# Attention row maxima turned by TensorE in f32 inside a product with V, and split from PSUM

## The chip, the cores and the metric

The kernel runs on one core of a Trainium2 chip. The metric is the device time of one execution in microseconds (us). TensorE (PE) multiplies matrices; VectorE (DVE), ScalarE (ACT) and GpSimd (POOL) compute; SyncE (SP) issues DMAs. Each engine runs its own list of instructions in order, and semaphores tie the lists together.

## The reference

```python
xn = _layernorm(x, axis=-1)                       # x: 8 x 512 x 512, f32
q, k, v = (proj(Wq), proj(Wk), proj(Wv))          # 16 heads of 32
q, k = _apply_rope(q, k)
scores = jnp.einsum('bhqd,bhkd->bhqk', q, k) / sqrt(32)
scores = jnp.where(causal, scores, finfo.min)
attn = jax.nn.softmax(scores, axis=-1)
out = jnp.einsum('bhqk,bhkd->bhqd', attn, v) ... @ Wo.T
# experts: top 2 of 8 by xn @ gate_w.T, softmax of the two as weights
y = sum over the two of (xn @ expert_w[e].T + expert_b[e]) * weight
return x + out + y
```

## The kernel before, in words

The attention is cut into 32 steps: one for each of 8 batches and 4 groups of 4 heads (`N = 32`). Step `n` on PE holds pieces of several steps' work, in an order written by hand in `step(n)`:

- `scores(n + 1, k)`, k = 0 to 10 (L959, L961): scores of the next step, queries on partitions, in two PSUM banks by turns. Their only use is the largest score of each row. `largest_score(n + 1, k)` on DVE (L1463) reduces each bank to columns of `top`, 128 partitions by 16 values (4 heads, 4 blocks of queries). Unit `k` waits until the maximum of unit `k - 2` is taken.
- `shifted_scores(n, k)`, k = 0 to 10 (L977): scores of this step the other way round, keys on partitions, with two more rows in the operands which subtract the row maximum. ACT takes the exponential of each (`exps`, L756) into `pT`. PE's unit waits for the exponential two units back.
- `times_v(n, j)` (L990, L993): exponentials by V, and by ones for the sums. It waits for `masked`: POOL zeroes the diagonal blocks (L590) when the exponentials of block j are there. `times_v(n, 0)` and `(n, 1)` are in step n, `(n, 2)` and `(n, 3)` in step n + 1.
- projections: Q and K of step n + 3 (L1027), V (L1036), the output projection (L1051). DVE rotates Q and K out of PSUM (L1447, L1448), POOL finishes them (L581, L582), ACT and POOL split them in two f16 halves (L741, L586), SP stores them and loads them back stacked.

The row maxima reach the two extra rows of Q in this way. After unit 10, `split_c` on DVE scales `top` by 2^-14 in f32 (L1471), again into f16 as the high half (L1472), and writes the difference as the low half (L1473): `c_hl`, 128 by 32 in f16. `turn_c` on PE (L966) turns it to 32 by 128 in PSUM; it stands behind `shifted_scores(n, 7)` and the last 6 passes of `project_v`. `copy_c` on ACT (L763), behind the eighth exponential, copies it to `c_turn`, 32 by 128. `move_c` on SP stores `c_turn` to memory (L411) and loads it as the two rows (L413). SP's later transfers of the step queue up behind `move_c`: K stored and stacked, and, at the head of the next step, in some steps the load of another batch of x.

Before step 0 the same is done once by a prologue with its own order. On DVE there: the last maxima, `split_c(0)`, `rotate(1, 2)`, `stats_of(1)` (layer norm of batch 1), `scale_of`, `rstd_of(1)`. On ACT there: `high_qk(1, 2)`, `copy_c(0)`, `take_v(1)`, `std_of(1)`, and `scale_x_for_pe(1)`, which waits for `rstd_of(1)`; then V tiles 2 and 3 are copied, for which PE's first `shifted_scores` waits.

Some steps carry more. In steps 2, 3, 5, 6, 8, 9 (`TURN_AT`) DVE turns four blocks of x (L1409), two of them among the last maxima. In steps 1, 2, 3, 5, 6, 8, 9, 10, 11 a weight matrix is split: `high_w` on ACT (L732) ahead of the eighth exponential and `low_w` on DVE (L1326). At step 11 (`CHOOSE`) DVE picks the experts (`choose(1)`, L1345 to L1354), and PE's `ranks` (L901) at the end of that step waits for it. Between steps 15 and 16 PE does the experts (L942). In steps 16 to 30 DVE adds experts' results to two output tiles a step (`add_experts`, L1507, L1508).

## Time and profile before

| | us |
|---|---|
| median of 3 runs | 1005.34 (1003.37, 1005.34, 1011.82) |
| the profiled execution's own time | 1008.12 |
| its span, first to last instruction | 1006.3 |
| PE busy | 932.0 |
| DVE busy | 743.2 |
| POOL busy | 565.7 |
| ACT busy | 435.2 |
| experts' stage on PE, about | 457 to 667 |

The granted TensorE clock was 0.982 of full on average. In the chain of work that ended last PE has 67%, DVE 12%, DMA 7%, POOL 6%. A step of the last stage, counted from the first `shifted_scores` of one step to that of the next, takes 21.05 us (841.14 to 862.19). Times in the rows are counted from the span's start; the duration of a row is from the first instruction's start to the last one's end, and PE's instructions overlap, so that the time a piece of PE's work takes is better read from start to start.

### The profile page before, as it was taken

How to read it: one execution, taken by the hardware profiler on the slowest of the kernel's cores; microseconds unless marked ns; L12 is line 12 of the kernel's file. 1: busy time of each engine (PE TensorE's matmuls, PEld its weight loads, DVE VectorE, ACT ScalarE, POOL GpSimd, SP SyncE). 2: the span in 40 equal slices, each digit the busy share in tenths (PEclk: the TensorE clock that was granted, in tenths of full speed). 3: DMA queues.
4: the chain of work that ended last, by engine and by line, in shares of the span. 5: the costliest groups of instructions: out<-in, count | busy, mean ns of one | idle time of the engine just before them, and what ended most of it. 6: DMA issues, size and time to landing. Idle time of an engine off the chain costs nothing.

```text
span 1006.3 us, 18752 instructions
## 1 busy us (share of the span) xinstructions
PE 932.0 (93%) x6589; PEld 447.7 (44%) x6589; DVE 743.2 (74%) x1322; ACT 435.2 (43%) x711; POOL 565.7 (56%) x557
## 2 busy tenths in 40 slices
PE   2899989989999978988999999989999999999887
PEld 1344434434444433444555555544444444444333
DVE  7888988888889899543444444477878888788865
ACT  5367866666765432331211211214433444334442
POOL 1545675664676548572333333237887788777651
PEclk9999999999999999998999999999999999999999
DMA  6366588788785352385555555554555554455431
GB/s 238 106 220 223 146 278 311 204 300 292 206 291 209 117 210 85 134 309 177 179 168 176 179 170 174 168 214 142 184 159 176 191 191 148 148 181 179 157 107 54
DMA packets 107964, 188.63 MB, mean 187 GB/s; under 512 B 11873, under 2 KB 65249, under 8 KB 102625
## 3 DMA queue, kind: packets, MB, share of 16 engines
q1 hardware_dynamic: 97072, 152.03, 44.5%
q0 software_dynamic: 10800, 35.40, 12.3%
q8 instruction: 56, 0.92, 0.4%
q14 instruction: 36, 0.29, 0.1%
HBM read 117.13 MB, written 70.25 MB: 186 GB/s over the span
## 4 chain that ended last, share of the span: by engine, by line
PE 67%; DVE 12%; DMA 7%; POOL 6%; ACT 4%; issue 3%; SPq 1%; another core or an unknown queue 0%; DVEq 0%; ACTq 0%; POOLq 0%
PE psum L942 18%; PE psum L1027 11%; PE psum L1036 6%; PE psum L1051 6%; PE psum L990 6%; PE psum L977 5%; PE psum L959 5%; PE psum L993 5%; DMA x_in<-x 3%; PE psum L919 3%; DVE top L1463 3%; PE psum L961 2%; POOL gT L571 1%; DMA c_rows<-c_turn 1%; POOL y_in L616 1%
## 5 line engine op out<-in xcount | busy, mean ns | idle before, releaser
L756 ACT ACTIVATE pT<-psum,factors 128x512 f32<-128x512 f32 (+1 forms) x352 | 219.6, 640 | 267.6 <-PE psum L977 239.3
L1463 DVE TENSOR_REDUCE top<-psum 128x1 f32<-128x384 f32 (+3 forms) x352 | 210.7, 635 | 24.1 <-PE psum L961 23.1
L1027 PE MATMUL psum<-xT,w_att 128*128 128x512 f16 x768 | 199.0, 385 | 6.9 <-DVE xT L1414 4.8
L942 PE MATMUL psum<-w_exp,x_gT 128*128 x852 | 197.4, 382 | 0.8 <-DVE x_gT L1419 0.6
L959 PE MATMUL psum<-k_stack,q_stack 96*128 96x384 f16 (+3 forms) x512 | 129.1, 305 | 22.2 <-DVE top L1463 21.4
L606 POOL DMA_INDIRECT x_g<-xn_rows,tok_of x71 | 67.3, 948 | 143.8 <-PE psum L919 136.4
L977 PE MATMUL psum<-q_stack,k_stack 98*128 98x256 f16 (+3 forms) x512 | 129.5, 306 | 6.3 <-ACT pT L756 5.0
L1419 DVE TENSOR_TENSOR x_gT<-psum,x_gT 128x512 f16<-128x512 f32 x71 | 49.0, 692 | 106.9 <-ACT x_gT L780 94.4
L942 PEld LDWEIGHTS psum<-w_exp,x_gT 128*128 128x128 f16 x852 | 83.9, 98 | 87.4 <-issue 3.9
L780 ACT ACTIVATE x_gT<-psum 128x512 f16<-128x512 f32 x71 | 42.3, 597 | 173.2 <-PE psum L919 173.1
L590 POOL TENSOR_SCALAR_AFFINE_SELECT pT<-pT 128x512 f32<-128x512 f32 x128 | 99.3, 785 | 18.7 <-ACT pT L756 18.7
L1027 PEld LDWEIGHTS psum<-xT,w_att 128*128 128x128 f16 x768 | 70.8, 99 | 75.2 <-issue 6.9
L990 PE MATMUL psum<-pT,v_sb 128*32 128x512 f32 (+1 forms) x992 | 93.3, 448 | 7.6 <-POOL pT L590 7.2
L596 POOL TENSOR_TENSOR o_hl<-o_sb,o_hl 128x512 f16<-128x512 f32 x31 | 36.5, 1176 | 112.0 <-ACT o_hl L770 112.0
L1051 PE MATMUL psum<-w_att,o_hl 128*128 128x512 f16 x384 | 98.1, 380 | 1.3 <-DVE o_hl L1500 1.3
L1036 PE MATMUL psum<-w_att,xT 128*128 128x512 f16 x384 | 98.6, 382 | 0.0
L993 PE MATMUL psum<-pT,ones 128*32 128x512 f32 (+1 forms) x992 | 90.4, 436 | 0.0
L961 PE MATMUL psum<-causal,ident 128*128 128x128 bf16 (+2 forms) x352 | 87.0, 247 | 0.0
L959 PEld LDWEIGHTS psum<-k_stack,q_stack 96*128 96x128 f16 x512 | 46.7, 98 | 78.2 <-DVE top L1463 40.3
L977 PEld LDWEIGHTS psum<-q_stack,k_stack 98*128 98x128 f16 x512 | 44.5, 98 | 80.4 <-issue 33.1
L616 POOL DMA_INDIRECT y_in<-y_rows,idx_y x64 | 66.0, 1032 | 19.7 <-issue 11.6
L1433 DVE SCALAR_TENSOR_TENSOR y_sb<-psum,down,bias_all 128x512 f32<-128x512 f32 x71 | 53.3, 751 | 17.7 <-issue 15.8
(172 smaller groups left out, 1283.9 us busy)
## 6 DMA issues: line engine op xcount, KB each, us to landing
y_rows<-y_sb SPq DMA_DIRECT2D x71, 256.0 KB
w_in<-w_all SPq DMA_DIRECT2D x12, 1024.0 KB, 9.6
q_stack<-qk_rows SPq DMA_DIRECT2D x96, 128.0 KB
k_stack<-qk_rows SPq DMA_DIRECT2D x96, 128.0 KB
x_in<-x SPq DMA_DIRECT2D x8, 1024.0 KB, 13.5
qk_rows<-q_hl SPq DMA_DIRECT2D x32, 256.0 KB, 2.2
qk_rows<-k_hl SPq DMA_DIRECT2D x32, 256.0 KB
xn_rows<-x_in SPq DMA_DIRECT2D x8, 1024.0 KB, 4.7
```

Of the source, the lines that this page charges most:

```text
L590: pool.affine_select(out=p_diagonal(j), in_=p_diagonal(j), compare_op=ALU.is_ge, fill=0.0, base=0, pattern=[[0, HG], [1, P]], channel_mult ...
L756: act.activation(p_of(j, h, heads), banks[BANK_T + (NT_ * n + k) % 2][:, 0:W], ACT.Exp, scale=factors[:, 0:1]).then_inc(exp_done, 1)
L942: now = pe.matmul(banks[s % 4], x_gT[s % 4][:, xp * C + c, :], w_exp[:, bass.ds(e, 1), wp, c, :].rearrange("p e d -> p (e d)"), start=n == ...
L959: pe.matmul(bank[:, h * W:(h + 1) * W], q_stack[u][0:ROW_C, h0 + h, i * P:(i + 1) * P], k_stack[u][0:ROW_C, h0 + h, 0:W], start=h == 0, st ...
L961: pe.matmul(bank[:, 0:heads * W].rearrange("p (h t) -> p h t", h=heads)[:, :, W - P:W], ident16[:], causal[:, 0:heads, :], start=False, st ...
L977: now = pe.matmul(bank[:, h * W:(h + 1) * W], k_stack[u][0:ROW_C + 2, h0 + h, j * P:(j + 1) * P], q_stack[u][0:ROW_C + 2, h0 + h, j * P:S] ...
L990: pe.matmul(banks[BANK_O][h * HD:(h + 1) * HD, j * P:S], v_sb[b % 2][:, j, g * P + h * HD:g * P + (h + 1) * HD], p_of(j, h, 1), start=j == ...
L993: now = pe.matmul(banks[BANK_DEN][h * HD:(h + 1) * HD, j * P:S], ones32[:], p_of(j, h, 1), start=j == 0, stop=j == J - 1)
L1027: now = pe.matmul(bank, w_att[:, what, wp, c, g * P:(g + 1) * P], xT[b % 2][:, xp * C + c, :], start=at_pass == 0, stop=at_pass == 3 * C - 1)
L1036: now = pe.matmul(banks[bank], xT[b % 2][:, xp * C + c, j * P:(j + 1) * P], w_att[:, 2, wp, c, :], start=at_pass == 0, stop=at_pass == 3 * ...
L1051: now = pe.matmul(banks[bank], o_hl[b % 2][:, c, xp, j * P:(j + 1) * P], w_att[:, 3, wp, c, :], start=at_pass == 0, stop=at_pass == 3 * C - 1)
L1463: return dve.tensor_reduce(out=top[:, h:h + heads, i], in_=banks[BANK_S + k % 2][:, 0:heads * W].rearrange("p (h t) -> p h t", h=heads), a ...
```

## The change

The split on DVE in front of the turn goes, with its three tiles `c_scale`, `c_f`, `c_hl`. PE turns `top` itself in f32 (16 by 128), inside `times_v(n, 0)`, behind the 4 products with V and ahead of the 4 with ones. ACT, now ahead of the eighth exponential, writes the high half from PSUM with the scale; DVE writes the low half from PSUM. `c_turn` becomes 16 by 2 by 128. DVE's `low_c` stands behind a block turn, a `low_w` or one tile of `add_experts` in the steps which have one, and directly behind the last maximum in the others.

```diff
-    c_turn = at("c_turn", [2 * HG * J, P], F16)
+    c_turn = at("c_turn", [HG * J, 2, P], F16)
...
             def move_c(m):
-                sp.wait_ge(c_copied, m + 1)
-                sp.dma_start(c_rows[m].rearrange("f (r t) -> (f r) t", t=P), c_turn[:]).then_inc(c_stored, 16)
+                sp.wait_ge(c_lo, m + 1)
+                sp.dma_start(c_rows[m].rearrange("f (r t) -> r f t", t=P), c_turn[:]).then_inc(c_stored, 16)
...
-            def copy_c(m):
+            def high_c(m):
                 act.wait_ge(c_turned, m + 1)
                 if m:
                     act.wait_ge(c_stored, 16 * m)
-                act.activation(c_turn[:], half(BANK_S + 1)[0:2 * HG * J, 0:P], ACT.Copy).then_inc(c_copied, 1)
+                act.activation(c_turn[:, 0, :], banks[BANK_S + 1][0:HG * J, 0:P], ACT.Copy, scale=2.0 ** -LOG_C).then_inc(c_hi, 1)
...
+                if n + 1 < N:
+                    high_c(n + 1)
                 exps(n, 7)
-                if n + 1 < N:
-                    copy_c(n + 1)
...
             def turn_c(m):
-                pe.wait_ge(c_made, m + 1)
-                pe.transpose(half(BANK_S + 1)[0:2 * HG * J, 0:P], c_hl[:].rearrange("p f r -> p (f r)"), ident16[:]).then_inc(c_turned, 1)
+                pe.wait_ge(max_done, NS * (m + 1))
+                pe.transpose(banks[BANK_S + 1][0:HG * J, 0:P], top[:].rearrange("p h i -> p (h i)"), ident32[:]).then_inc(c_turned, 1)
...
+                if j == 0 and n + 1 < N:
+                    turn_c(n + 1)
                 for h in range(HG):
                     now = pe.matmul(banks[BANK_DEN][h * HD:(h + 1) * HD, j * P:S], ones32[:], p_of(j, h, 1),
...
-                if nxt:
-                    turn_c(n + 1)
                 shifted_scores(n, 8)
...
-            def split_c(m):
-                dve.wait_ge(max_done, NS * (m + 1))
-                if m:
-                    dve.wait_ge(c_turned, m)
-                tops = top[:].rearrange("p h i -> p (h i)")
-                dve.tensor_tensor(c_f[:], tops, c_scale[:], ALU.mult)
-                own.link(dve.tensor_tensor(c_hl[:, 0, :], tops, c_scale[:], ALU.mult))
-                dve.tensor_tensor(c_hl[:, 1, :], c_f[:], c_hl[:, 0, :], ALU.subtract).then_inc(c_made, 1)
+            def low_c(m):
+                dve.wait_ge(c_hi, m + 1)
+                dve.scalar_tensor_tensor(c_turn[:, 1, :], banks[BANK_S + 1][0:HG * J, 0:P], 2.0 ** -LOG_C, c_turn[:, 0, :],
+                                         ALU.mult, ALU.subtract).then_inc(c_lo, 1)
...
                     largest_score(n + 1, 10)
-                    split_c(n + 1)
                 if n in TURN_AT:
                     turn_blk(TURN_AT[n], 2)
+                elif n - 1 in JOB_AT:
+                    low_w(JOB_AT[n - 1])
+                for w in late_tiles(n)[:1]:
+                    add_experts(w)
+                if nxt:
+                    low_c(n + 1)
+                if n in TURN_AT:
                     turn_blk(TURN_AT[n], 3)
                 if n == CHOOSE:
                     choose(1)
-                if n - 1 in JOB_AT:
+                if n in TURN_AT and n - 1 in JOB_AT:
                     low_w(JOB_AT[n - 1])
...
-            split_c(0)
             rotate(1, 2)
+            low_c(0)
             stats_of(1)
```

On DVE in the prologue, before the first step, the order was this (each name is the tile written, then what it is read from; `stats` is `stats_of(1)`):

```order
L1463 TENSOR_REDUCE top<-psum 128x1 x7
L1471 TENSOR_TENSOR c_f<-top,c_scale 128x16
L1472 TENSOR_TENSOR c_hl<-top,c_scale 128x16
L1473 TENSOR_TENSOR c_hl<-c_f,c_hl 128x16
L1447 STREAM_SHUFFLE turned_k<-psum 128x512
L1448 TENSOR_TENSOR plain_k<-psum,trig_sb 128x512
L1286 BN_STATS stats<-x_in_143 128x6 x4
```

and is now this (the file's lines are 3 to 7 fewer for the same code):

```order
L1460 TENSOR_REDUCE top<-psum 128x1 x7
L1444 STREAM_SHUFFLE turned_k<-psum 128x512
L1445 TENSOR_TENSOR plain_k<-psum,trig_sb 128x512
L1465 SCALAR_TENSOR_TENSOR c_turn<-psum,c_turn 16x128
L1283 BN_STATS stats<-x_in_139 128x6 x4
```

The write of the low half, which waits for ACT, stands in front of the statistics of batch 1; the three instructions of the split waited for DVE alone.

On PE around `times_v(n, 0)` the order was:

```order
L1036 MATMUL psum<-w_att,xT_136 128x512 x3
L990 MATMUL psum<-pT,v_sb_103 32x512 x4
L993 MATMUL psum<-pT,ones_54 32x512 x4
L977 MATMUL psum<-q_stack_97,k_stack_100 128x384
L1036 MATMUL psum<-w_att,xT_136 128x512 x6
L966 MATMUL psum<-ident_49,c_hl 32x128
L977 MATMUL psum<-q_stack_97,k_stack_100 128x256 x4
```

and is now:

```order
L1035 MATMUL psum<-w_att,xT_133 128x512 x3
L987 MATMUL psum<-pT,v_sb_100 32x512 x4
L963 MATMUL psum<-ident_50,top 16x128
L992 MATMUL psum<-pT,ones_54 32x512 x4
L974 MATMUL psum<-q_stack_94,k_stack_97 128x384
L1035 MATMUL psum<-w_att,xT_133 128x512 x6
L974 MATMUL psum<-q_stack_94,k_stack_97 128x256 x4
```

The turn is now ahead of the products with ones, one `shifted_scores` and six passes of `project_v`.

On DVE at the end of step 11 (`best` to `gap` is `choose(1)`, `w_hl` is `low_w`) the order was:

```order
L1463 TENSOR_REDUCE top<-psum 128x1 x2
L1471 TENSOR_TENSOR c_f<-top,c_scale 128x16
L1472 TENSOR_TENSOR c_hl<-top,c_scale 128x16
L1473 TENSOR_TENSOR c_hl<-c_f,c_hl 128x16
L1345 TENSOR_REDUCE best<-rest 128x32
...
L1353 TENSOR_TENSOR chosen<-one_hot_152,one_hot_153 128x256
L1354 TENSOR_TENSOR gap<-best 128x32
L1326 SCALAR_TENSOR_TENSOR w_hl<-w_in_140,up,w_hl 128x2048
```

and is now:

```order
L1460 TENSOR_REDUCE top<-psum 128x1 x2
L1323 SCALAR_TENSOR_TENSOR w_hl<-w_in_137,up,w_hl 128x2048
L1465 SCALAR_TENSOR_TENSOR c_turn<-psum,c_turn 16x128
L1342 TENSOR_REDUCE best<-rest 128x32
...
L1350 TENSOR_TENSOR chosen<-one_hot_149,one_hot_150 128x256
L1351 TENSOR_TENSOR gap<-best 128x32
```

The choice of experts stands behind the low half of a weight matrix and of the maxima, and no longer ahead of it.

## Rows read from the trace of the kernel before

**Rows 1.** A stretch: its us; busy PE, PEld, DVE, ACT, POOL (instructions); PE clock; DMA.

```profile
693.00:925.00 232.00, 232.00 (x1732) 106.98 (x1728) 193.33 (x320) 98.72 (x176) 184.77 (x187) 1.00 0.55 172
```

**Rows 2.** Waits, whole run: us in total, times, longest.

```profile
PE psum L959 <- DVE top L1463: 21.4, 15, 3.1
```

**Rows 3.** Timeline of PE in step 24: start us, us, instruction.

```profile
849.65 1.06 PE L990 MATMUL psum<-pT,v_sb 128*32 128x512 f32 x8
850.53 1.04 PE L993 MATMUL psum<-pT,ones 128*32 128x512 f32 x8
851.51 0.34 PE L977 MATMUL psum<-q_stack,k_stack 98*128 98x384 f16 x1
851.68 1.46 PE L1036 MATMUL psum<-w_att,xT 128*128 128x512 f16 x6
853.07 0.23 PE L966 MATMUL psum<-ident,c_hl 128*32 128x128 f16 x1
853.23 0.39 PE L977 MATMUL psum<-q_stack,k_stack 98*128 98x256 f16 x2
```

**Rows 4.** Timeline of PE around an f32 turn ahead of 32-wide products.

```profile
246.95 0.27 PE L896 MATMUL psum<-ident,amax 128*128 128x128 f32 x1
247.15 0.64 PE L990 MATMUL psum<-pT,v_sb 128*32 128x256 f32 x8
```

**Rows 5.** Groups by line and shape: count, busy us, mean ns, idle before.

```profile
L1473 DVE TENSOR_TENSOR c_hl<-c_f,c_hl 128x16 f16<-128x16 f32 x32 | 33.6, 1051 | 1.1
...
L1471 DVE TENSOR_TENSOR c_f<-top,c_scale 128x16 f32<-128x16 f32 x32 | 13.2, 412 | 1.1
...
L1472 DVE TENSOR_TENSOR c_hl<-top,c_scale 128x16 f16<-128x16 f32 x32 | 5.2, 163 | 0.0
```

**Rows 6.** Timeline of the prologue: DVE, ACT, PE; idle time and its releaser in brackets.

```profile
53.94 2.46 DVE L1286 BATCH_NORM_STATS2 stats<-x_in 128x6 f32<-128x512 f32 x4
...
57.28 0.25 ACT L763 ACTIVATE c_turn<-psum 32x128 f16<-32x128 f16 x1
...
59.45 2.92 ACT L698 ACTIVATE x_p<-x_in,shift,rstd 128x512 f32<-128x512 f32 x4 [1.14 <-DVE shift L1302]
...
63.40 0.39 PE L977 MATMUL psum<-q_stack,k_stack 98*128 98x512 f16 x1 [1.08 <-ACT v_sb L748]
```

**Rows 7.** Timeline of step 11: ACT's high half of a weight, DVE's choice, PE's ranks.

```profile
326.59 2.00 ACT L732 ACTIVATE w_hl<-w_in,up 128x2048 f16<-128x2048 f32 x1
...
328.23 0.41 DVE L1345 TENSOR_REDUCE best<-rest 128x32 f32<-128x256 f32 x1
...
331.62 0.43 DVE L1353 TENSOR_TENSOR chosen<-one_hot,one_hot 128x256 f16<-128x256 f32 x1
...
334.53 0.95 PE L901 MATMUL psum<-chosen,ones 128*128 128x8 f16 x32
```

**Rows 8.** Timeline of step 5: PE's product with ones, DVE, POOL.

```profile
187.32 1.04 PE L993 MATMUL psum<-pT,ones 128*32 128x512 f32 x8
...
187.42 0.65 DVE L1463 TENSOR_REDUCE top<-psum 128x1 f32<-128x512 f32 x1
...
191.00 2.30 DVE L1326 SCALAR_TENSOR_TENSOR w_hl<-w_in,up,w_hl 128x2048 f16<-128x2048 f32 x1
...
192.09 2.23 POOL L586 TENSOR_TENSOR k_hl<-plain_k,k_hl 128x512 f16<-128x512 f32 x1 [1.68 <-ACT k_hl L741]
```

**Rows 9.** The chain that ended last, pieces in order: start us, us, what.

```profile
144.11 4.34 DMA c_rows<-c_turn
...
154.78 15.12 DMA x_in<-x
```

**Rows 10.** Timeline of step 24: DVE, POOL, and PE's second product with V.

```profile
848.80 1.28 DVE L1463 TENSOR_REDUCE top<-psum 128x1 f32<-128x512 f32 x2
...
853.54 1.08 POOL L590 TENSOR_SCALAR_AFFINE_SELECT pT<-pT 128x512 f32<-128x512 f32 x1
...
855.73 0.85 PE L990 MATMUL psum<-pT,v_sb 128*32 128x384 f32 x8
```

More of the change, by code:

```diff
@@ L123, in moe_attention_layer @@
     top = at("top", [P, HG, J], F32)
-    c_scale = at("c_scale", [P, HG * J], F32)
-    c_f = at("c_f", [P, HG * J], F32)
-    c_hl = at("c_hl", [P, 2, HG * J], F16)
-    c_turn = at("c_turn", [2 * HG * J, P], F16)
+    c_turn = at("c_turn", [HG * J, 2, P], F16)
     rden_few = at("rden_few", [P, S // HD], F32)
@@ L233, in moe_attention_layer @@
     v_summed, v_read, qk_factor, vo_factor = (sem(n) for n in ("v_summed", "v_read", "qk_factor", "vo_factor"))
-    s_done, max_done, c_made, c_turned, c_copied, c_stored = (sem(n) for n in ("s_done", "max_done", "c_made", "c_turned", "c_copied", "c_stored"))
+    s_done, max_done, c_turned, c_hi, c_lo, c_stored = (sem(n) for n in ("s_done", "max_done", "c_turned", "c_hi", "c_lo", "c_stored"))
     c_loaded = [sem(f"c_loaded{u}") for u in range(3)]
@@ L850, in _ @@
             act.wait_ge(qk_factor, 1)
-            copy_c(0)
+            high_c(0)
             take_v(1, V_FIRST[1])
@@ L956, in scores @@
                 elif m:
-                    pe.wait_ge(c_copied, m)
+                    pe.wait_ge(c_lo, m)
                 for h in range(heads):
@@ L1131, in step @@
                 if not nxt:
-                    pe.wait_ge(c_copied, N)
+                    pe.wait_ge(c_lo, N)
                     project_out(N - 2, OUT_LAST[2], 0, 6)
@@ L1261, in _ @@
             pe.wait_ge(max_done, NS * (N1 + 1))
-            pe.wait_ge(c_copied, N1 + 1)
+            pe.wait_ge(c_lo, N1 + 1)
             pe.wait_ge(exp_done, NT_ * N1)
@@ L1604, in step @@
                     spread_low(1, 1)
-                for w in late_tiles(n):
+                for w in late_tiles(n)[1:]:
                     add_experts(w)
-            own.link(dve.memset(c_scale[:], 2.0 ** -LOG_C))
             for u in range(2):
```

## The prediction

> **What bounds the kernel now.** I read the busy time by stretch first. Through steps 17 to 27 PE is busy for all of 232.00 us at the full clock, while DVE is busy for 193.33 of them [rows 1]. There the time is PE's own work, and what DVE is spared buys nothing. Then the waits: over the whole run PE loses 21.4 us before scores because a maximum is not yet taken [rows 2], nearly all of it in steps 1 to 15, 29 and 30. That is the most a faster DVE could return. Last the timelines around each place where the change puts or moves an instruction, since it moves waits as well as work.
>
> **PE's own work.** The old turn costs PE 0.27 us: six passes from 851.68, 0.214 us apart ((1.46 - 0.39) / 5), are through at 852.96, and the next `shifted_scores` starts at 853.23 [rows 3]. For the new one, a 16-wide f32 turn between 32-wide products, there is no row. The nearest is an f32 turn ahead of the same 32-wide products: 0.20 us from start to start (246.95 to 247.15) [rows 4]. From below it could cost nothing: four 32-wide products run at once (four of 512 columns take the 0.88 us from 849.65 to 850.53, [rows 3]) and the turn uses one of the four column groups. From above it pays the change of width twice: going back from 32-wide products to a full-width one costs 0.10 us more than going on (0.98 us from 850.53 to 851.51 against 0.88), so 0.30. I take 0.20: -0.07 us in each of 31 steps, **-2.2 us**, with ends of -8.4 and +0.9.
>
> **DVE's work.** The split takes 33.6 + 13.2 + 5.2 = 52.0 us in 32 calls, 1.6 us each, most of it the last instruction, 1051 ns for 16 columns [rows 5]. `low_c` I put at 0.3 us: between the 163 ns of the 16-column instruction [rows 5] and half of the 0.65 us of a 512-column read of PSUM [rows 8]. That makes 42 us less on DVE. In steps 17 to 27 it is worth nothing [rows 1]. In the steps with no work between the last maximum and `low_c` (0, 4, 7, 12 to 15) DVE now waits there for PE's turn and ACT's high half, about 1 us, so the saving is a few tenths at most. In the others it ends the tail earlier, and most of those tails are followed by a wait of DVE for PE. What is left of it is in the gains below.
>
> **The prologue.** `low_c(0)` stands ahead of `stats_of(1)`, which started at 53.94 [rows 6]. It waits for `high_c(0)` on ACT, which stays behind `high_qk(1, 2)`: the copy in its place ran from 57.28 to 57.53 [rows 6], and nothing that it waits for comes more than 0.25 us sooner. So DVE stands still from about 53.6, writes the low half by 57.65, and the statistics start 3.7 us later. They feed `rstd_of(1)`, ACT's x_p (59.45, released by DVE), the V tiles and PE's first `shifted_scores` (63.40), which waits for these tiles already, 1.08 us [rows 6]. No slack lies on this path: **+3.7 us**. The ends are +3.7 and, should ACT or PE make some of it up, 0.
>
> **Step 11.** `choose(1)` takes 3.8 us (328.23 to 332.05), and PE's ranks start at 334.53, 2.5 us after it [rows 7]. Now `low_w` stands ahead of it. That waits for ACT's high half, ready at 328.59 [rows 7], and takes 2.3 us at best [rows 8]; with `low_c` behind it the choice starts at 331.2 and ends at 335.0, or 0.5 later if `low_w` is slowed. PE waits 0.5 to 1.0 us: **+0.8 us** (ends 0 and +1.5).
>
> **The turn's wait on PE.** PE now needs all maxima at the end of the products with V. In step 24 they end at 850.08 and PE comes to the place at 850.53 [rows 3, 10]: 0.45 us to spare, and no wait. In the six steps with block turns among the maxima they are late: in step 5 the last ends at 188.07, and PE started the products with ones at 187.32 [rows 8]. PE waits 0.75 us plus a semaphore, 0.85. In steps 3 and 6 that is covered, since PE waits over 2 us for DVE later. In steps 2, 5, 8 and 9 PE later waits for POOL's half of x, and this chain gets shorter: POOL's k_hl took 2.23 us beside DVE's `low_w`, which ran from 191.00 to 193.30 [rows 8]; `low_w` now ends about 1 us earlier, and k_hl starts later, so that the 1.2 us in which they overlapped (192.09 to 193.30) should be mostly saved. I take +0.2 us each, **+0.8 us** (ends 0 and +3.4).
>
> **Gains elsewhere.** The rows leave up to 2 us earlier. In the first stage SP's chain carries this on: the store took 4.34 us at 144.11, and behind it SP came to issue the load of x at 154.78, which landed 15.12 us later and held DVE [rows 9]; PE gets back under 1 us there and about 0.4 at step 8. ACT's new order spares one copy (0.25 us, [rows 6]) between the last V pass and the ninth exponential, for which PE waits in four steps without an output projection. With the smaller waits behind a shorter tail, **-2.0 us** (ends -5 and 0).
>
> The sum is -2.2 + 3.7 + 0.8 + 0.8 - 2.0 = **+1.1 us**. The profiled execution took 1008.12 us (span 1006.3), so 1009.2; the median of the runs shown is 2.8 lower, and gives **1006.5 us**.
>
> **Weighed against the Trainium skill.** The turn's price rests on rows 3 and 4. The Trainium skill, TensorEngine Tiling (Array Packing), sections Restrictions and Key Properties, says that column tiling shuts off transpose mode for f32 input, and that a change of tiling mode drains the engine. By it the turn is either an ordinary f32 product in one column group or a full-width one with a drain on both sides, and no run here shows which. By the drain the sum would be the first rival's; by the value from rows it is the forecast.
>
> **The rivals.**
> - *The turn in f32 makes PE drain* (chance 0.13). The array changes width ahead of it and again behind. The turn then costs the upper bound of 0.30 us, 31 x 0.10 on top of the forecast: 1009.6. For it: the 0.10 at each change of width [rows 3]. Against: the old turn was 32 wide too, and 16 columns fit in one group.
> - *POOL gets late, slower than before* (0.12). With the split gone, `add_experts` moves 1.6 us forward into POOL's work on K. Its instructions read two tensors in SBUF, and so did the split's last one, whose 1051 ns for 16 columns are time held up by POOL [rows 5]; POOL's mask of block 1 took 1.08 us, and ended at 854.62, and PE needs it at 855.73 [rows 10]. The slack is 1.11 us. If each of POOL's three instructions ahead of that is held for a further 0.5 us, PE waits 0.4 us a step in the 14 steps from 16 on, +5.6: 1012. It decides from 1.11 us of added delay on. Against: the split held POOL too, and two instructions of it are gone.
> - *DVE's relief comes through* (0.20). Of the 21.4 us [rows 2] PE gets 6 back in the first stage, and the turn is nearly hidden: 1000. For it: the prologue is the only place where the new wait is long. Against: the long waits of steps 12 to 14 come from DVE work in the same step, behind a point where DVE waited for PE.
> - *More than that* (0.06): turn hidden, -8.4, and over 8 us of the waits gone: below 995.
> - *Several added waits, all at their upper ends, beyond 1%* (0.04): 3.7 + 1.5 + 3.4 + 0.9 and POOL's 5.6 make 1020.
>
> The forecast itself, all terms near the values taken, gets 0.45.
>
> **Range and chances.** 999 to 1012 us: it takes in the forecast (about 1003 to 1010), the drain, most of POOL's rival and most of the relief. A measurement of this kernel can tell 1% (10 us) from no change. Faster by over 1%: 0.06. Slower by over 1%: 0.05. Within: 0.89.
>
> **What would show it.** Right: DVE idle for near 3.7 us in front of the first low half, and the first `shifted_scores` near 67 us; an idle gap of some 0.8 us on PE ahead of the new turn in steps 2, 3, 5, 6, 8 and 9 and none in steps 17 to 27; ranks of step 11 released by DVE; a step of the last stage 0.0 to 0.1 us under 21.05 us. Wrong: a last-stage step over 21.05 (the drain if PE shows no wait, POOL if the second product with V waits for a mask); or a first stage that, prologue aside, is shorter by over 4 us, which would say that DVE bounded more of it than the waits tell.

## The result

The changed kernel takes 1017.27 us in the median of 4 runs (1015.32 to 1019.23) against 1006.84 for the kernel before beside it; the ratio is 1.0098, 95% interval 1.0056 to 1.0140. A second comparison, on another chip, gave 1016.80 us against 1008.28, ratio 1.0072 (1.0039 to 1.0106). So it is slower, by 0.7% to 1%, and lies outside the 999 to 1012 us that were forecast around 1006.5. The profiled run of the change took 1017.24 us (span 1015.4), that of before 1008.12 (span 1006.3): 9.1 us to explain, where the working had a sum of 1.1.

Call the time from the first `shifted_scores` of one step to that of the next the length of the step. (Line numbers behind the edit are 3 to 7 lower in the changed kernel: L956 and L958 the scores, L974 the shifted scores, L987 and L992 the product with V and its sums, L963 the turn, L760 `high_c`, L1465 `low_c`.) Between the two profiles the 9.1 us lie like this:

```
stretch                           before    after   differs  forecast
up to step 0                       63.40    65.84     +2.44      +3.7
step 0                             22.87    25.55     +2.68      -0.1
steps 1 to 10                     231.38   234.46     +3.08      -1.9
step 11                            24.29    25.69     +1.40      +0.7
steps 12 to 16 (experts in 15)    351.83   350.28     -1.55      -0.3
steps 17 to 30                    286.00   286.96     +0.96      -1.0
last step                          26.54    26.63     +0.09       0
```

The last column spreads the working over the stretches: -0.07 us a step for the turn, +3.7 in the prologue, +0.8 in step 11, and +0.8 and -2.0 in steps 1 to 10. One profile stands against one here. Steps 1 to 10 took 231.53 us in another profile with the split in place (experiment 2), and 233.5 to 234.5 in four others with the change's prologue and steps (experiments 3 and 6, and the change again), so their +3.1 is no accident of one profile. With the prologue alone mended and the same ten steps they took 232.0 and 233.3 (experiments 1 and 8): some of it hangs on the late start. It lies in steps 3, 4 and 6 (+0.85, +0.90, +1.25). The stretch of steps 12 to 16 scatters more: two profiles of one kernel (experiment 7) differ there by 3.6 us.

**The last stage.** The changed kernel's stretch first, read as [rows 1], then PE's timeline in its step 24:

```profile
702.00:925.00 223.00, 223.00 (x1628) 101.32 (x1627) 182.47 (x291) 97.25 (x171) 177.54 (x180) 1.00 0.56 172
```

```profile
858.29 1.06 PE L987 MATMUL psum<-pT,v_sb 128*32 128x512 f32 x8
859.28 0.28 PE L963 MATMUL psum<-ident,top 128*16 128x128 f32 x1
859.49 1.06 PE L992 MATMUL psum<-pT,ones 128*32 128x512 f32 x8
860.49 0.34 PE L974 MATMUL psum<-q_stack,k_stack 98*128 98x384 f16 x1
```

PE is still busy for all of the stretch, though DVE's share of it fell. From the first product with V to the next shifted scores it is 2.20 us, and was 1.86 [rows 3]: the turn takes 0.34 us without waiting for anything. The old one took 0.27. A step of this stage lasts 21.13 us instead of 21.05.

**The prologue.** Timelines of DVE (two rows), ACT and PE, around the low half's new place; brackets are idle time and what ended it:

```profile
56.57 0.28 DVE L1465 SCALAR_TENSOR_TENSOR c_turn<-psum,c_turn 16x128 f16<-16x128 f32 x1 [3.73 <-ACT c_turn L760]
56.78 2.45 DVE L1283 BATCH_NORM_STATS2 stats<-x_in 128x6 f32<-128x512 f32 x4
...
56.29 0.25 ACT L760 ACTIVATE c_turn<-psum 16x128 f16<-16x128 f32 x1
...
61.90 2.93 ACT L695 ACTIVATE x_p<-x_in,shift,rstd 128x512 f32<-128x512 f32 x4 [0.76 <-DVE shift L1299]
...
63.16 0.39 PE L956 MATMUL psum<-k_stack,q_stack 96*128 96x256 f16 x2 [2.22 <-DVE top L1460]
...
65.84 0.61 PE L974 MATMUL psum<-q_stack,k_stack 98*128 98x512 f16 x1 [1.69 <-ACT v_sb L745]
```

DVE stands still for 3.73 us in front of `low_c(0)`, as forecast; the statistics start at 56.78, not 53.94 [rows 6]. PE passes the delay on twice, 2.22 and 1.69 us. Behind that the granted clock is lower. The same stretch, before and then after, columns as in [rows 1]:

```profile
64.00:72.00 8.00, 8.00 (x53) 4.85 (x51) 6.54 (x14) 6.95 (x12) 3.12 (x3) 1.00 0.77 274
```

```profile
64.00:72.00 8.00, 6.31 (x25) 3.37 (x24) 3.08 (x7) 5.26 (x9) 0.00 (x0) 0.57 0.69 259
```

0.57 is a stretch spent mostly at the 1.2 GHz level: the first product of step 0 takes 0.61 us where its like took 0.39 [rows 6], and step 0 lasts 2.68 us longer.

The clock differs in two more places, and both enter the table. Before and then after for the first, after for the second:

```profile
21.00:28.00 7.00, 4.83 (x12) 1.79 (x13) 6.13 (x5) 1.38 (x1) 0.00 (x0) 0.53 0.00 0
```

```profile
21.00:28.00 7.00, 4.78 (x14) 1.80 (x15) 6.28 (x7) 1.44 (x1) 0.00 (x0) 1.00 0.00 0
...
231.00:236.00 5.00, 4.91 (x73) 2.72 (x72) 3.67 (x12) 0.32 (x2) 0.00 (x0) 0.66 0.97 310
```

In the prologue PE stood for 4.83 us before and for 4.66 after, until 23.2 us in both, and was granted the lower level in the one profile (0.53) and the upper in the other (1.00); DVE's first rotation of Q then starts at 27.90 us instead of 28.56. That 0.66 us is not the change's: with `low_c` out of the way the profiles at the lower level start step 0 at 62.98 to 63.13 (experiments 7, 8 and 9), those at the upper one at 62.21 to 62.64 (experiments 1, 7, 10 and 12). In step 6 the clock falls after a wait of 3.10 us for a maximum; the kernel before keeps the upper level in all of steps 1 to 10.

**The waits, the low half, and step 11.** The first two rows are PE's waits of the whole run, the next DVE's and the group of `low_c` by shape, and the last are DVE and PE in step 11:

```profile
PE psum L956 <- DVE top L1460: 23.5, 16, 3.1
...
PE psum L963 <- DVE top L1460: 5.0, 6, 1.5
```

```profile
DVE c_turn L1465 <- ACT c_turn L760: 17.7, 12, 3.7
...
L1465 DVE SCALAR_TENSOR_TENSOR c_turn<-psum,c_turn 16x128 f16<-16x128 f32 x32 | 8.8, 275 | 17.9 <-ACT c_turn L760 17.7
```

```profile
336.85 3.11 DVE L1323 SCALAR_TENSOR_TENSOR w_hl<-w_in,up,w_hl 128x2048 f16<-128x2048 f32 x1 [2.04 <-ACT w_hl L729]
...
343.58 0.42 DVE L1350 TENSOR_TENSOR chosen<-one_hot,one_hot 128x256 f16<-128x256 f32 x1
...
344.15 0.94 PE L898 MATMUL psum<-chosen,ones 128*128 128x8 f16 x32 [1.16 <-DVE chosen L1350]
```

PE's wait for maxima before scores did not shrink (21.4 before, [rows 2]; 2.2 of the 23.5 are the prologue's) and 5.0 us ahead of the turn came on top. `low_c` takes 275 ns, so DVE works 43.2 us less on the rows than the 52.0 of [rows 5], but stands still 17.7 us for ACT to write the high half. In step 11 the ranks wait 1.16 us for the choice.

**The store.** The rows leave earlier and arrive no earlier where transfers are dense. A piece of the chain of waits around step 4:

```profile
170.15 0.22 PE psum L963
170.39 0.28 ACT c_turn L760
170.69 0.29 DVE c_turn L1465
171.00 9.57 DMA c_rows<-c_turn
```

From the last maximum to the store's issue it is 1.48 us here and was 3.54. From there to the load behind it, which waits for it, it took 9.6 us in place of 5.8. SP had issued the 1 MB store of normalised x 0.68 us ahead of it, and 2.77 us ahead of it before; that such transfers held it up is my reading. Over steps 2 to 9 the time from the last maximum to that load adds up to 54.4 us before and to 54.4 after. The new form of the store isn't the reason: with it, but issued late (experiment 9), the time from store to load in steps 1 to 10 is 33.6 us in all, against 35.9 before and 45.9 in the change.

### The profile page after: what moved, and what is told of

Its sections match the earlier page's. It is cut to its first block, busy times and chain, and to the rows that moved or that the text cites. A ratio compares the mean times of both kernels' runs of the same rounds, so it can differ in the third digit from the quotient of the medians.

```text
span 1015.4 us, 18656 instructions
## 1 busy us (share of the span) xinstructions
PE 936.7 (92%) x6589; PEld 448.0 (44%) x6589; DVE 710.6 (70%) x1257; ACT 439.2 (43%) x711; POOL 567.9 (56%) x557
## 4 chain that ended last, share of the span: by engine, by line
PE 66%; DVE 11%; DMA 9%; POOL 6%; ACT 3%; issue 2%; SPq 2%; DVEq 0%; ACTq 0%; POOLq 0%
PE psum L939 18%; PE psum L1026 10%; PE psum L1050 6%; PE psum L987 6%; PE psum L992 5%; PE psum L974 5%; PE psum L1035 5%; PE psum L956 5%; PE psum L916 4%; DMA x_in<-x 3%; DVE top L1460 2%; PE psum L958 2%; DMA c_rows<-c_turn 2%; DMA x_blk<-xn_rows 1%; POOL plain_q L579 1%
## 5 line engine op out<-in xcount | busy, mean ns | idle before, releaser
L956 PE MATMUL psum<-k_stack,q_stack 96*128 96x384 f16 (+3 forms) x512 | 129.2, 305 | 24.5 <-DVE top L1460 23.5
L974 PE MATMUL psum<-q_stack,k_stack 98*128 98x256 f16 (+3 forms) x512 | 128.9, 306 | 6.2 <-ACT pT L753 4.3
L587 POOL TENSOR_SCALAR_AFFINE_SELECT pT<-pT 128x512 f32<-128x512 f32 x128 | 103.8, 821 | 23.7 <-ACT pT L753 23.5
L987 PE MATMUL psum<-pT,v_sb 128*32 128x512 f32 (+1 forms) x992 | 94.0, 452 | 10.1 <-POOL pT L587 10.1
L992 PE MATMUL psum<-pT,ones 128*32 128x512 f32 (+1 forms) x992 | 92.1, 444 | 0.0
L958 PE MATMUL psum<-causal,ident 128*128 128x128 bf16 (+2 forms) x352 | 86.9, 247 | 0.0
L974 PEld LDWEIGHTS psum<-q_stack,k_stack 98*128 98x128 f16 x512 | 46.9, 98 | 85.1 <-issue 33.2
L956 PEld LDWEIGHTS psum<-k_stack,q_stack 96*128 96x128 f16 x512 | 46.6, 98 | 80.8 <-DVE top L1460 47.1
L613 POOL DMA_INDIRECT y_in<-y_rows,idx_y x64 | 62.2, 972 | 19.7 <-issue 11.1
L578 POOL TENSOR_TENSOR turned_q<-turned_q,trig_sb 128x512 f32<-128x512 f32 x32 | 42.9, 1341 | 48.0 <-DVE plain_q L1445 48.0
```

The lines of the kernel that those rows point to most:

```text
L587: pool.affine_select(out=p_diagonal(j), in_=p_diagonal(j), compare_op=ALU.is_ge, fill=0.0, base=0, pattern=[[0, HG], [1, P]], channel_mult ...
L956: pe.matmul(bank[:, h * W:(h + 1) * W], q_stack[u][0:ROW_C, h0 + h, i * P:(i + 1) * P], k_stack[u][0:ROW_C, h0 + h, 0:W], start=h == 0, st ...
L958: pe.matmul(bank[:, 0:heads * W].rearrange("p (h t) -> p h t", h=heads)[:, :, W - P:W], ident16[:], causal[:, 0:heads, :], start=False, st ...
L974: now = pe.matmul(bank[:, h * W:(h + 1) * W], k_stack[u][0:ROW_C + 2, h0 + h, j * P:(j + 1) * P], q_stack[u][0:ROW_C + 2, h0 + h, j * P:S] ...
L987: pe.matmul(banks[BANK_O][h * HD:(h + 1) * HD, j * P:S], v_sb[b % 2][:, j, g * P + h * HD:g * P + (h + 1) * HD], p_of(j, h, 1), start=j == ...
L992: now = pe.matmul(banks[BANK_DEN][h * HD:(h + 1) * HD, j * P:S], ones32[:], p_of(j, h, 1), start=j == 0, stop=j == J - 1)
```

## The experiments

Each is timed against the kernel before on the same chip. Experiments 5, 10 and 11 have one execution each and are read by the length of their steps alone. The expectations count units from 0: their seventh exponential is `exps(n, 7)`, the eighth in order, and their eighth shifted scores `shifted_scores(n, 8)`.

**1. The prologue alone mended.**

```
             rotate(1, 2)
-            low_c(0)
             stats_of(1)
             scale_of(NJ)
+            low_c(0)
```

> The changed kernel with one line moved: in the prologue VectorE writes the low half of the first maxima behind the statistics and scale of batch 1 and no longer ahead of them. Theory A (the prologue's wait is the largest single loss, 3.2 us of standing still plus the half clock that follows it from 64.43 to 71.26 us, about 2.7 us): the first shifted_scores starts 3 us earlier, the granted clock stays at its full level through 64 to 72 us, and the kernel is 5 to 6 us faster than the changed one, about 1011 us. Theory B (the loss is made in the steps, by waits of VectorE and by stores that queue behind bulk transfers): the 3 us return but are taken back at a later wait for a load of x; 1015 to 1017 us.

Measured: 1010.44 us, ratio 1.0041 (1.0015 to 1.0067). DVE and then PE:

```profile
52.55 2.47 DVE L1283 BATCH_NORM_STATS2 stats<-x_in 128x6 f32<-128x512 f32 x4
...
56.50 0.27 DVE L1465 SCALAR_TENSOR_TENSOR c_turn<-psum,c_turn 16x128 f16<-16x128 f32 x1
```

```profile
62.21 0.39 PE L974 MATMUL psum<-q_stack,k_stack 98*128 98x512 f16 x1 [0.91 <-ACT v_sb L745]
```

Step 0 starts at 62.21, 3.6 us ahead of the change, and lasts 22.92. It is also 1.2 us ahead of before, but DVE was 0.9 us ahead already at its first rotation of Q (27.67 us against 28.56), with PE's clock from 21 to 28 us as the difference; the shorter DVE work has the rest. About half of the loss was here.

**2. The same wait put into the kernel before**, and nothing else.

```
             rotate(1, 2)
+            dve.wait_ge(c_copied, 1)
             stats_of(1)
```

> The kernel before with one wait added: in the prologue VectorE waits for ScalarE's copy of the turned maxima ahead of the statistics of batch 1, as the change makes it do; nothing else of the change is in it. Theory A: first shifted_scores 3 us later, half clock after it, 5 to 6 us slower than before, about 1011 to 1012 us. Theory B (a delay there is absorbed later): under 2 us slower.

Measured: 1010.89 us, ratio 1.0044 (1.0019 to 1.0070). Step 0 starts at 67.79 and lasts 25.61, 7.1 us lost by step 1; the steps 17 to 27 stay at 21.05. Put in, the wait alone costs 0.4%; taken out (experiment 1), it gave back 0.3% to 0.6%, by which of the change's two ratios one takes.

**3. PE kept busy in its two waits**, ten and eight products of 512 columns whose sums are overwritten, run twice.

```
+                if n == 0:
+                    pe.wait_ge(amax_read, 4)
+                    keep_busy(10)
                 if nxt:
                     scores(n + 1, 2)
...
                 if n == 0:
+                    keep_busy(8)
                     pe.wait_ge(v_read, 4)
```

> The changed kernel with 18 products added on TensorE at the start of step 0 (10 ahead of the third unit of scores, 8 ahead of the first shifted_scores), whose results nothing reads: they fill the time in which TensorE waits because of the prologue. Theory A (the half clock from 64.43 us on comes from TensorE's idle time there, and costs by itself): the first shifted_scores starts where it did in the changed kernel, near 65.8 us, the granted clock stays at its full level, and step 0 takes 2 to 3 us less than the 25.55 us of the changed kernel. Theory C (step 0 is long for another reason, such as late maxima or DMAs): step 0 stays within 0.5 us of 25.55.

> The changed kernel with products that nobody uses (their sums are overwritten) filling PE's two waits at the end of the prologue, 10 and 8 of 512 columns, so that PE never stands. In the one profile so far the granted clock then stays full from 64 to 72 us, and step 0 goes from 25.55 to 22.92 us, with the start of step 0 up to 0.9 us later. Theory: the 1.7 to 2.6 us gained there are half given back in the experts' stage, as every late arrival has been, and the median is 1 to 1.5 us below the changed kernel. Rival: they come through in full, 2 to 2.6 us below. Third: below 0.5 us, all absorbed, so the half clock in step 0 has no part in the result.

> The changed kernel, unchanged, to have it beside the next one on the same chip. Ratio 1.0098 so far with an interval of 1.0056 to 1.014: expected 1.008 to 1.011.

```profile
64.00:72.00 8.00, 7.90 (x46) 4.08 (x45) 5.07 (x11) 7.13 (x12) 0.95 (x1) 1.00 0.80 280
```

This is the first profile; the clock stays at its upper level and step 0 is 22.92 us long in both. It starts at 66.7 to 66.8, later than the 65.84 of the change, as PE had the lower level from 21 to 28 us in both. Yet the ratios are 1.0105 (1.0066 to 1.0145) and 1.0097 (1.0062 to 1.0132), beside 1.0098 and 1.0072 for the change. The rival that the half clock has no part in the result comes nearest. In the profiles beside each other (second comparison) the 2.1 us won by step 1 are 1.0 at step 17; the spans are 1013.7 and 1015.7. So no cost of the clock behind the late start was measured in the time; with intervals of this width one or two microseconds cannot be excluded.

**4. The turn behind the sums** instead of ahead of them.

```
-                if j == 0 and n + 1 < N:
-                    turn_c(n + 1)
                 for h in range(HG):
                     now = pe.matmul(banks[BANK_DEN]...
                 now.then_inc(pv_done, 1)
+                if j == 0 and n + 1 < N:
+                    turn_c(n + 1)
```

> The changed kernel with the turn moved from between the products with V and those with ones to behind both. Theory A (the turn costs 0.34 us because the array goes from 32-wide to another width and back, and the maxima are late in six steps): only one change of width is left beyond those that are there anyway, so a step of the last stage goes from 21.13 back to 21.0 us or less, and the idle time of TensorE ahead of the turn (5.0 us in 6 places) is under 0.5 us, since the place comes 0.9 us later; 3 to 6 us faster than the changed kernel. Theory B (a turn of 16 columns in f32 costs 0.3 us wherever it stands): last-stage steps stay at 21.13 us and only the waits of the six steps go, 1 to 3 us.

```profile
858.19 1.06 PE L987 MATMUL psum<-pT,v_sb 128*32 128x512 f32 x8
859.07 1.04 PE L990 MATMUL psum<-pT,ones 128*32 128x512 f32 x8
860.04 0.28 PE L963 MATMUL psum<-ident,top 128*16 128x128 f32 x1
860.16 0.33 PE L974 MATMUL psum<-q_stack,k_stack 98*128 98x384 f16 x1
```

Measured: 1014.11 us, ratio 1.0084 (1.0051 to 1.0117). Here the whole stretch takes 1.97 us, 0.11 more than without a turn [rows 3]. Steps 17 to 24 last 20.89 us: 0.24 less than in the change, 0.16 less than before. PE's waits ahead of the turn are gone, all six. The time alone doesn't show the 3 to 6 us expected: the ratio lies between the change's 1.0072 and 1.0098.

**5. The turn issued twice**, at the change's place.

```
                 pe.wait_ge(max_done, NS * (m + 1))
+                pe.transpose(banks[BANK_S + 1][0:HG * J, 0:P], top[:]..., ident32[:])
                 pe.transpose(banks[BANK_S + 1][0:HG * J, 0:P], top[:]..., ident32[:]).then_inc(c_turned, 1)
```

> The changed kernel with each turn of the 16 columns issued twice, one right behind the other, at the same place between the product with V and its sums. It tells apart what makes the turn cost 0.34 us there (the V products' first start to the first shifted scores is 2.20 us against 1.86 without it). A: the columns written change from 32 wide to 16 and back, and the two changes cost 0.23; the turn alone streams in 0.11, as it does behind the sums (860.04 to 860.16 in that kernel). Then a second turn adds 0.11, and a step from 17 to 24 goes from 21.13 to 21.24 us, all twelve of them to +1.3 us. B: every f32 turn costs 0.34 where it stands, whatever its neighbours. Then a second one adds 0.34, and the step is 21.47. Between 21.30 and 21.40 would leave both partly right. Forecast: 21.24 (A, 0.75).

Measured: the step is 21.25 us, 0.11 to 0.12 longer. The second turn costs only what it streams; the rest of the 0.34 is paid once, around them.

**6. Choice first in step 11.**

```
-                elif n - 1 in JOB_AT:
+                elif n - 1 in JOB_AT and n != CHOOSE:
                     low_w(JOB_AT[n - 1])
...
-                if n in TURN_AT and n - 1 in JOB_AT:
+                if (n in TURN_AT or n == CHOOSE) and n - 1 in JOB_AT:
```

> The changed kernel with one order put back: in step 11 VectorE makes the choice of experts before it splits the weights, as in the kernel before, so that the ranks on PE don't wait for it. Theory: step 11 is 1.4 us shorter (25.69 to 24.29) and the later steps do not take it back before the experts; there a late arrival has so far been half recovered (1.5 to 4 us of it in step 15), so the median goes from 1017.3 to 1016.3, by 0.7 to 1.4 us. Rival: the wait just moves, the split of the weights then holds up step 12, and step 11 and 12 together stay at 50.2 us; the median stays at 1017.

Measured: step 11 lasts 24.38 us instead of 25.69, step 12 24.04 instead of 24.47, so the wait does not just move. The median is 1014.19 us, ratio 1.0065 (1.0038 to 1.0092), but the runs reach from 1009.26 to 1019.55 and the time alone does not tell 1.3 us.

**7. All three mended (1, 4 and 6 together)**, run twice.

> The changed kernel with all three faults mended: no wait of VectorE ahead of the statistics in the prologue, the turn behind the sums of the V product instead of ahead of them, the choice of experts first in step 11. Theory: the gains add up. The prologue alone gave 1010.4, the turn behind the sums takes 0.24 us off each of some 25 steps that PE bounds, of which the median showed 3.2, the choice up to 1.4, half taken back by the experts' stage: 1006.5, within 1 us of the kernel before (1006.1). The steps 17 to 24 last 20.89 against 21.05 before. Rival: what the prologue and the turn gained is the same time, given back where the experts' stage waits for its transfers, and it stays at 1009 to 1010. Third: it is faster than before by over 2 us (1004), because the steps 17 to 27 alone give 1.8 and nothing is lost elsewhere; chance 0.2.

> The kernel with all three mended once more, unchanged: its ratio to the kernel before was 0.9974 with an interval of 0.9947 to 1.0001, too near to 1. Theory: the steps 17 to 27 alone are 1.8 us shorter than before and steps 1 to 16 break even, so the ratio is 0.9975 to 0.9985 and the interval excludes 1. Rival: it was the draw of the runs, and it is 1.000 within 0.002.

Measured: 1006.66 us, ratio 0.9974 (0.9947 to 1.0001), and 1007.96 us, ratio 0.9996 (0.9971 to 1.0022). Together the three take away the whole loss, and in time the kernel equals the one before.

**8. The same with the turn at the change's place** (1 and 6 only).

> The changed kernel with the prologue's wait gone and the choice first, but the turn where the change has it, between the product with V and its sums. Against the kernel with all three mended it differs by 0.24 us in each step, and by nothing else. Theory: the steps 17 to 27 cost 0.24 times 10, and step 28 to 30 up to 0.3 more, 2.7 us in the last stage, and the steps 1 to 16 one or two more: 1009.5 to 1010.5. Rival: the waits of stage one swallow the 0.24 there and the experts' stage takes back the rest, and only the 2.7 of the last stage stay: 1009.

Measured: 1010.56 us, ratio 1.0013 (0.9982 to 1.0043), steps 17 to 24 21.14 us. As forecast in size, but the intervals of 7 and 8 overlap; what the place costs is shown by the steps, 0.25 us each.

**9. All three mended, with the turn at the old place.**

```
                 if vs:
                     project_v(n + G, BANK_QV, 6, 12)
+                if nxt:
+                    turn_c(n + 1)
                 shifted_scores(n, 8)
```

> As the kernel with all three mended, but with the turn at the old place: ahead of the eighth shifted scores, between products of 128 columns, with ScalarE's copy behind the seventh exponential as before. Only the form of the turn (f32, 16 columns, split from PSUM) and VectorE's relief are then left of the change. A (the width decides): the turn stands between 128 columns and 128, pays both changes of width, 0.34 us instead of 0.11, and a step from 17 to 24 lasts 21.12 us against 20.89 with the turn behind the sums; the median is about 1009.5, 3 us above the kernel with all three mended. B (the place between the product with V and its sums was the fault, not the width): the turn costs 0.11 here too, the step lasts 20.9, and the median is within 1 us of the kernel with all three mended. Beside it: if the early start of the store was worth something in steps 3 to 14, this kernel is slower there by 1 us or more in sum; by my reading the transfers land no earlier, and it is not.

```profile
857.34 1.46 PE L1033 MATMUL psum<-w_att,xT 128*128 128x512 f16 x6
858.64 0.27 PE L963 MATMUL psum<-ident,top 128*16 128x128 f32 x1
858.75 0.38 PE L974 MATMUL psum<-q_stack,k_stack 98*128 98x256 f16 x2
```

ScalarE's copy stands behind `exps(n, 7)` here too, which the cut above doesn't show. Measured: 1009.45 us, ratio 1.0007 (0.9988 to 1.0026); steps 17 to 24 last 20.90 us. Theory A falls: between products of 128 columns the turn costs 0.11 as well. Right in total, wrong in its reason: the time was lost in the first stage. There steps 1 to 10 take 238.4 us in place of the 233.1 with the turn behind the sums, and in that stretch DVE stands still 18.3 us ahead of `low_c` for the later high half. With the same copy and the turn behind the sums (experiment 12, two profiles) these waits are 12.1 and 15.5 us, and the ten steps take 233.5 and 232.5; the turn's place is all that differs. The longer waits of DVE are a likely cause, and not shown to be the only one: the granted clock is a little lower too (0.97 against 0.98 and 0.99).

**10. The same, with 32 columns turned.** The maxima's tile gets 16 columns of zeros beside it, and their rows are read by nobody.

```
-    top = at("top", [P, HG, J], F32)
+    top = at("top", [P, 2 * HG, J], F32)
...
-                pe.transpose(banks[BANK_S + 1][0:HG * J, 0:P], ...
+                pe.transpose(banks[BANK_S + 1][0:2 * HG * J, 0:P], ...
```

> As the kernel with the turn at the old place, but 32 columns are turned instead of 16: 16 columns of zeros beside the maxima, and nobody reads their rows. What makes a turn dear? By the runs so far the f32 turn of 16 columns costs 0.11 between products of 128 columns and behind the sums of 32, and 0.34 between two runs of products of 32 columns, while the f16 turn of 32 columns cost 0.25 (0.09 ahead of it, 0.16 behind) between products of 128. A: the chip counts a stationary operand of 32 columns as another form than one of 128, and one of 16 as the same as 128; each change costs about 0.1. Then this turn costs 0.11 and two changes, 0.31 to 0.34, and a step from 17 to 24 lasts 21.10 to 21.13. B: it is the type (f16 among f16 products costs, f32 does not) or the f32 turn as such: it costs 0.11 as with 16 columns, and the step stays at 20.90. Forecast: A, 0.7.

```profile
857.62 0.27 PE L963 MATMUL psum<-ident,top 128*32 128x128 f32 x1
857.73 0.38 PE L974 MATMUL psum<-q_stack,k_stack 98*128 98x256 f16 x2
```

Measured: 0.11 us again, step 20.90 us. The width of the turn does not matter; the forecast (A) fell.

**11. An f16 turn between the product with V and its sums**, added to the kernel before, which keeps its own.

```
+                if j == 0 and n + 1 < N:
+                    pe.wait_ge(max_done, NS * (n + 2))
+                    pe.transpose(half(BANK_S + 1)[0:2 * HG * J, 0:P], ident16[:, 0:2 * HG * J], ident16[:])
                 for h in range(HG):
                     now = pe.matmul(banks[BANK_DEN]...
```

> The kernel before, plus a second turn that nobody uses: an f16 turn with 32 columns (of the identity), between the product with V and its sums, where the change has its f32 turn; the real turn stays at its old place. What is to be explained: an f32 turn of 16 columns costs 0.34 us there, and 0.11 ahead of the eighth shifted scores, with 32 columns as well as with 16; the f16 turn of 32 columns costs 0.25 ahead of the eighth shifted scores. A: products whose stationary operand has 32 columns run in another mode than those of 128, a change of mode costs 0.1 in either direction, an f16 turn of 32 columns is in the 32-column mode and an f32 turn, however wide, in the full one. Then the f16 turn pays no change between the product with V and its sums, and costs what it streams, 0.05: product to sums goes from 0.88 to 0.93 or 0.95, and a step from 17 to 24 from 21.05 to 21.10 us. B: whatever stands between those two runs breaks them up, for 0.2 and more: product to sums 1.1 to 1.2, step 21.3. Forecast: A, 0.7.

```profile
853.60 1.06 PE L990 MATMUL psum<-pT,v_sb 128*32 128x512 f32 x8
854.48 0.22 PE L994 MATMUL psum<-ident 128*32 128x128 f16 x1
854.49 1.07 PE L996 MATMUL psum<-pT,ones 128*32 128x512 f32 x8
855.49 0.34 PE L977 MATMUL psum<-q_stack,k_stack 98*128 98x384 f16 x1
```

Measured: from the first product to the shifted scores 1.89 us against 1.86 [rows 3], step 21.09 against 21.05. An f16 turn costs 0.03 to 0.04 us in the very place where the f32 one costs 0.34: theory A.

**12. All three mended, and ScalarE's copy behind the eighth exponential as before**, run twice.

```
-                if n + 1 < N:
-                    high_c(n + 1)
                 exps(n, 7)
+                if n + 1 < N:
+                    high_c(n + 1)
```

> As the kernel with all three mended, with the turn behind the sums, but ScalarE's copy (and with it the store of the rows) behind the seventh exponential as before. The kernel with the turn at the old place had steps of 20.90 us too, and was still 2.8 us slower in the median; in its trace steps 4, 5, 8 and 10 together were 4.5 us longer. Theory A: the early store is what those steps gain by (it leaves at 1.0 to 1.5 us after the last maximum instead of 2.6, and the loads behind it in SyncE's queue with it), so this kernel gives the gain back and stands at 1008.5 to 1009.5. B: what counts is where the turn stands on PE (the eighth shifted scores no longer wait behind it), and this kernel stays at 1006.5. Forecast: A, 0.6.

> The kernel with all three mended and ScalarE's copy behind the seventh exponential, once more: its ratio was 0.9972 (0.9949 to 0.9994). The steps 17 to 27 last 20.89 us against 21.05, 1.8 us in all; that alone is 0.998. Expected 0.997 to 0.999; chance that the interval again excludes 1: 0.5.

Measured: 1005.48 us, ratio 0.9972 (0.9949 to 0.9994), and 1003.54 us, ratio 0.9947 (0.9924 to 0.9969). Theory A falls: the store leaves 0.6 us later than in experiment 7 (2.97 us behind the last maximum instead of 2.33 in the steps without block turns), and nothing is lost by it. This is the one version faster than both kernels, than the one before by 0.3% to 0.5%. The 1.8 us that the expectation gives to steps 17 to 27 are 1.4: step 25 lasts 21.2 us here, the other ten 20.89.

## Why the prediction was wrong

Measured less forecast, the error of 8.0 us in the sum is +5.0 in steps 1 to 10, +2.8 in step 0, +2.0 in steps 17 to 30, +0.7 in step 11, and -1.3 each in the prologue and in steps 12 to 16. The largest part stands where the gains elsewhere were forecast, and none came. (From 1009.2 less 2.8 the forecast should read 1006.4; that changes nothing.)

- **The turn's price**, the step "I take 0.20", failed: 0.34 us, above the upper bound of 0.30, so that the -2.2 us of 31 steps became +0.08 each, 1.0 us in steps 17 to 27. The row it rested on was the start-to-start time from an f32 turn to a product of 32 columns [rows 4]: it holds one change, between a turn and 32-column products. Between two runs of them the turn pays two. The rows of 4, 5, 9, 10 and 11 fit one reading, and fit no other that I tried: products with a 32-column stationary operand run in another mode than the rest, each change costs PE 0.09 to 0.12 us (0.98 against 0.88 in [rows 3], 0.97 in experiment 4; 0.99, 0.21 and 1.00 from the turn's row on in the change, where 0.88, 0.11 and 0.88 are the work), an f16 turn of 32 columns belongs to that mode, and an f32 turn of 16 or of 32 to the full one. The f16 turn of the kernel before stood between 128-column products and paid both changes: 0.11 ahead of it (852.96 to 853.07) and 0.16 from its start to the next (853.07 to 853.23), 0.05 of that its own [rows 3]. The f32 turn needs 0.11 of its own. The upper bound failed because it gave the turn itself only 0.10 beside two changes.
- **Weighed against the Trainium skill**: TensorEngine Tiling (Array Packing), sections Restrictions and Key Properties, says that column tiling shuts off f32 transpose mode and that a change of tiling mode drains the engine. The times agree: PE pays 0.10 to 0.11 us on either side of the turn; experiments 10 and 11 are what tells type from width. That what PE pays there is a drain, no run here shows. The rival built on it had the mechanism and not the size.
- **The prologue** was right in mechanism and place (DVE 3.73 us idle, forecast 3.7) and near in size when priced by the time: 4.4 us, 1.0044, for the wait alone. Step 0 started at 65.84, not near 67. The working said that nothing ACT waits for would come more than 0.25 us sooner; the copy ran at 56.29 in place of 57.28. Of that 1.0 us 0.66 was luck, the clock of 21 to 28 us, and the rest the shorter split. The half clock in step 0 was overlooked too and put 2.68 us into the profile, but no gain in time was measured where it was taken away (experiment 3).
- **Gains elsewhere, -2.0 us**, failed. Steps 1 to 10 lost 3.1 us where -1.9 was forecast, and in none of the kernels with `low_c` did they fall below the 231.4 us of before: 232.0 in the best, 238.4 in the worst profile (two profiles of one kernel were 233.1 and 235.0). Two things are seen where the relief should have arrived: DVE stands still for ACT's high half, and the store that leaves earlier lands no earlier. By experiment 12 the last 0.6 us of the earlier store are worth nothing.
- **The turn's wait on PE** was forecast at six places with 0.85 us each, and came at six, 5.0 us in all (0.61 to 1.5). The working took +0.8 us net. Experiment 11 has the same wait in the kernel before (4.6 us in the same six steps), and its steps 1 to 10 last 233.8 us: 2.4 more than before, of which its ten f16 turns explain 0.4. So the wait was priced too low there, with one profile for it, in which the clock was also lower for 3.4 us.
- **Step 11**: ranks released by DVE, as forecast; +1.4 us against +0.8, within its bounds. `low_w` took 3.11 us, the working had 2.3 at best.
- **POOL late** did not occur in steps 17 to 27: its mask in step 24 ended 0.9 us ahead of the product that needs it. Over the whole run PE's waits for masks grew from 7.2 to 10.1 us: 2.7 in step 13, where there were none, and 0.9 more in step 16. Step 24, POOL and then PE:

```profile
862.47 1.08 POOL L587 TENSOR_SCALAR_AFFINE_SELECT pT<-pT 128x512 f32<-128x512 f32 x1
```

```profile
864.45 0.85 PE L987 MATMUL psum<-pT,v_sb 128*32 128x384 f32 x8
```

- **DVE's relief comes through** was wrong: of 43 us, 0.3 to 0.4 reached the start of step 0 (62.98 to 63.13 against 63.40 at the same clock), and none is seen in steps 1 to 10. What the best version gains in steps 17 to 24, 0.16 us each, is PE's: two changes of mode saved, less 0.06 us more streaming.

The 3.1 us lost in steps 1 to 10 can be split only in part: PE stands 1.1 us longer (19.5 us against 18.4) and is busy 1.9 us longer, of which the turn has about 0.8, and the 3.4 us at the 1.2 GHz level can have up to 1.7. What let the clock fall, beyond the wait just before, is not shown. The last version gains more than the 1.4 us of steps 17 to 27, and its cause isn't shown: in its two profiles 3.0 and 3.7 us of the 4.8 lie in steps 12 to 16. Step 15, with the experts, lasts between 239.0 and 243.2 us in these profiles, and the kernel before has the longest; that stays open, and does not go with how late it starts. The granted clock goes with much of the scatter of one kernel: over the 23 executions of the kernel before beside experiment 1, the time falls by 0.6 us for each 0.001 of mean clock (correlation -0.87).

## What to carry to other kernels

Before moving a product on PE, write down the mode of its neighbours: a turn in f32 costs 0.11 us next to full-width products or at the end of a run of 32-column ones, and three times that in the middle of one. An instruction that now waits for another engine has to be looked at where everything is serial, in the prologue, first: that one wait cost 0.4%, and the 43 us taken off DVE, which was not the bound, gave next to nothing for it. A store sent earlier need not land earlier: look at when the load behind it starts. And before two profiles are compared stretch by stretch, compare their granted clocks: here 0.66 us of the prologue was the clock's.

## What the runs showed of the hardware

- A change between products of 32 columns and full-width ones costs PE 0.09 to 0.12 us at the upper clock; f16 turns of 32 columns are on the one side of it, f32 turns of 16 or 32 on the other.
- An f32 turn of 128 rows streams in 0.11 us, an f16 one between 32-column products in 0.03 to 0.04.
- After waits of 2.22 and 1.69 us with some work between them PE was granted the 1.2 GHz level (0.57 as the mean of 64 to 72 us); with the waits filled by products nobody uses it kept 2.4 GHz (1.00), and no gain in time was measured.
- Around waits of 4.83 and of 4.66 us at the same place in two kernels (until 23.2 us) PE was granted 0.53 and 1.00 of its clock from 21 to 28 us, and what followed was 0.66 us apart.
- From the issue of a store of 16 x 2 x 128 f16 to that of the load behind it, which waits for it, it took between 1.3 and 9.6 us.
